# Cross-attention and mixture of experts: routed chunks of 64 tokens as two passes of 32 over four column tiles, the hidden block turned on VectorE

## What is computed

```python
x = x + xattn(layernorm(x), ctx, ctx, mask, ...)      # attention over 77 context rows
h = layernorm(x).reshape(-1, 256)
shared = (silu(h @ shared_gate) * (h @ shared_up)) @ shared_down
logits = h @ gate_w
topk_ids, topk_val = argmax(logits, -1), max(logits, -1)
xs = h * sigmoid(topk_val)[:, None]
# every token goes to the one expert e = topk_ids[token]
routed = (silu(xs @ routed_gate[e]) * (xs @ routed_up[e])) @ routed_down[e]
out = x + (shared + routed).reshape(x.shape)
```

## Time and profile before

| | |
|---|---|
| time, median of 3 runs | 328.64 us (328.41 to 329.23) |
| the profiled execution | 326.08 us, span of its instructions 324.1 us |
| granted TensorE clock | 0.982 of full speed over the span |
| TensorE busy | 89% of the span |
| VectorE, ScalarE, GpSimd busy | 39%, 27%, 16% |
| chain that ended last | TensorE 74%, VectorE 8%, issue 5% |

### The profile page before, as it was taken

One profiled execution on the slowest core, in us unless ns is written; L12 is line 12 of the kernel. 1 busy time (PEld: TensorE's weight loads), 2 busy tenths in 40 slices (PEclk: granted clock), 3 DMA queues, 4 the chain that ended last, 5 costly groups with the idle time before them and its releaser, 6 DMA issues.

```text
span 324.1 us, 7366 instructions
## 1 busy us (share of the span) xinstructions
PE 288.6 (89%) x2502; PEld 194.8 (60%) x2503; DVE 127.5 (39%) x402; ACT 88.2 (27%) x224; POOL 50.4 (16%) x88
## 2 busy tenths in 40 slices
PE   4968899987989999899999899989999989999760
PEld 3735665533834885567766676757776756764450
DVE  1648868773993211332223222222323222222423
ACT  2157764442211023322221222222222212221000
POOL 1245212110077400000000000000000000001772
PEclk9999999999999999999999999999999999999895
DMA  6999999000023351268885869999948995105475
GB/s 200 351 373 372 372 370 374 24 1 2 0 82 109 113 181 36 74 253 269 318 286 169 259 194 328 383 366 378 358 152 266 344 375 189 32 0 129 129 223 166
DMA packets 55148, 69.69 MB, mean 215 GB/s; under 512 B 4030, under 2 KB 37211, under 8 KB 55131
## 3 DMA queue, kind: packets, MB, share of 16 engines
q1 hardware_dynamic: 46203, 61.60, 55.7%
q10 hardware_dynamic: 7392, 3.67, 4.6%
q0 software_dynamic: 1536, 4.20, 4.2%
HBM read 59.49 MB, written 9.96 MB: 214 GB/s over the span
## 4 chain that ended last, share of the span: by engine, by line
PE 74%; DVE 8%; issue 5%; POOL 4%; DMA 3%; ACT 3%; ACTq 1%; POOLq 0%; SPq 0%; DVEq 0%
PE bank L991 29%; PE bank L1005 13%; PE bank L914 12%; PE bank L1015 6%; PE bank L926 4%; POOL xs_flat L436 4%; PE bank L845 3%; DMA slot_rows<-late 1%; DVE h_place L504 1%; PE bank L880 1%; DVE h_place L505 1%; ACT h_place L715 1%; DMA xs_flat<-slot_rows,slot_i 1%; DMA h_place<-in_L_xattn_kernel_q_dram 1%; PE bank L863 1%
## 5 line engine op out<-in xcount | busy, mean ns | idle before, releaser
L991 PE MATMUL bank<-ring_gu,h_place 128*64 128x256 f32 x784 | 95.4, 385 | 5.0 <-issue 4.5
L991 PEld LDWEIGHTS bank<-ring_gu,h_place 128*64 128x64 f32 x784 | 53.9, 136 | 34.8 <-issue 15.1
L616 DVE COPY h_place<-xs_flat 128x128 f32 x50 | 11.4, 227 | 104.2 <-PE bank L991 100.9
L1005 PE MATMUL bank<-ring_d,h_place 128*64 128x128 f32 x784 | 51.4, 273 | 0.5 <-ACT h_place L755 0.5
L1005 PEld LDWEIGHTS bank<-ring_d,h_place 128*64 128x64 f32 x784 | 46.6, 137 | 7.2 <-ACT h_place L755 0.8
L436 POOL DMA_INDIRECT xs_flat<-slot_rows,slot_i x16 | 15.6, 978 | 191.9 <-DMA slot_rows<-late 187.4
L755 ACT COPY h_place<-bank 128x256 f32<-128x256 f32 x49 | 18.2, 372 | 83.7 <-PE bank L1015 83.7
L926 PE MATMUL bank<-shd,h_place 128*128 128x256 f32 x128 | 30.0, 395 | 2.2 <-issue 2.2
L926 PEld LDWEIGHTS bank<-shd,h_place 128*128 128x128 f32 x128 | 25.3, 199 | 7.2 <-issue 3.5
L750 ACT ACTIVATE h_place<-bank 128x256 f32<-128x256 f32 x49 | 18.8, 383 | 38.8 <-PE bank L991 38.8
L914 PE MATMUL bank<-late,shg 128*128 128x512 f32 x48 | 23.1, 603 | 4.3 <-DVE h_place L505 4.2
(11 more groups left out here) (132 smaller groups left out, 246.9 us busy)
## 6 DMA issues: line engine op xcount, KB each, us to landing
ring_gu<-L_ffn_routed_gate_w_dram SPq DMA_DIRECT2D x32, 512.0 KB, 5.9
ring_gu<-n_L_ffn_routed_up_w_dram SPq DMA_DIRECT2D x32, 512.0 KB, 7.0
ring_d<-L_ffn_routed_down_w_dram SPq DMA_DIRECT2D x32, 512.0 KB, 6.6
slot_rows<-late ACTq DMA_DIRECT2D x14, 256.0 KB, 4.4
x<-in_x_dram SPq DMA_DIRECT2D x4, 512.0 KB, 7.1
slot_rows<-zeros SPq DMA_DIRECT2D x1, 2048.0 KB, 14.4
late<-sorted_rows SPq DMA_DIRECT2D x8, 256.0 KB, 3.4
out_dram<-x SPq DMA_DIRECT2D x8, 256.0 KB
```

The source lines that it names most:

```text
L991: ins = te.matmul(bank[w][a * LW:(a + 1) * LW, 0:FH], x_c[:, k], ring_gu[:, s, w, k, a * FH:(a + 1) * FH], start=(k == 0), stop=(k == KD - 1))
L1005: ins = te.matmul(bank[4][a * LW:(a + 1) * LW, 0:DH], hT[:, mp, mh * LW:(mh + 1) * LW], ring_d[:, s, m, a * DH:(a + 1) * DH], start=(m == ...
```

## The change

Gate/up is split by tokens: two passes u = 0, 1 of 32 tokens, each into a bank of its own, over four column tiles. Tile q gets the columns with index m * 128 + q * 32 + f (m = 0 to 3, f = 0 to 31) of gate and of up side by side, so that bank u holds on partition q * 32 + t the gate of token t in its left 128 columns and the up in the next 128. After silu and product on 128x128 blocks, a transposition within 32x32 blocks (VectorE, `turn`) gives `hT` with the hidden index on the partitions. The transposes on TensorE, bank 3 and the copy `keep_hT` go; ScalarE takes over `take_y`. Down runs as four column tiles of 32 (two halves of the output, two halves of the tokens). `x_c` stays a single buffer, `hT` too; `h_r` and silu's output have one buffer for each pass.

```diff
 def take_x(c):
     col = dve.value_load(begin[0:1, bass.ds(c, 1)], min_val=0, max_val=T)
-    dve.wait_ge(u_done, HALVES * c)
+    dve.wait_ge(gu_done, HALVES * c)
     v.tensor_copy(x_c, xsT[:, :, bass.ds(col, LW)]).then_inc(x_ready, 1)
-def gated(c):
-    dve.wait_ge(silu_done, c + 1)
-    dve.wait_ge(u_done, HALVES * (c + 1))
-    v.tensor_tensor(h_r, h_r, bank[1][:, 0:FH], ALU.mult).then_inc(h_ready, 1)
-def take_y(c):
-    dve.wait_ge(down_done, HALVES * (c + 1))
-    v.tensor_copy(y_all[:, bass.ds(c, 1)].rearrange("p c d -> p (c d)"), bank[4][:, 0:DH]).then_inc(y_ready, 1)
+def gated(c, u):
+    dve.wait_ge(silu_done, HALVES * c + u + 1)
+    v.tensor_tensor(h_r[u], g_silu[u], bank[u][:, P:2 * P], ALU.mult).then_inc(h_ready, 1)
+def turn(c, u):
+    dve.wait_ge(h_ready, HALVES * c + u + 1 + FREE2)
+    v.transpose(hT[:, :, u * LU:(u + 1) * LU],
+                h_r[u].rearrange("p (m f) -> p m f", m=KF)).then_inc(hT_ready, 1)
...
 with dve.Fori(1, n_chunks) as c:
+    for u in range(HALVES):
+        dve.wait_ge(hT_ready, HALVES * c + u - 1)
+        gated(c, u)
     take_x(c + 1)
-    gated(c)
-    take_y(c - 1)
-take_y(n_chunks - 1)
+    dve.wait_ge(down_done, c)
+    for u in range(HALVES):
+        turn(c, u)
...
 def silu(c):
-    act.wait_ge(g_done, HALVES * (c + 1))
-    act.wait_ge(hT_done, c)
-    a_.activation(h_r, bank[0][:, 0:FH], ACT.Silu).then_inc(silu_done, 1)
-def keep_hT(c):
-    act.wait_ge(hT_done, c + 1)
-    act.wait_ge(down_done, HALVES * c)
-    a_.copy(hT.rearrange(FLAT), bank[3][:, 0:FH]).then_inc(hT_ready, 1)
+    for u in range(HALVES):
+        act.wait_ge(gu_done, HALVES * c + u + 1)
+        act.wait_ge(h_ready, HALVES * c + u + 1)
+        a_.activation(g_silu[u], bank[u][:, 0:P], ACT.Silu).then_inc(silu_done, 1)
+def take_y(c):
+    act.wait_ge(down_done, c + 1)
+    a_.copy(y_all[:, bass.ds(c, 1)].rearrange("p c d -> p (c d)"), bank[4][:, 0:DH]).then_inc(y_ready, 1)
...
 def gate_up(c, s):
     pe.wait_ge(x_ready, c + 1)
-    for w, done in ((0, g_done), (1, u_done)):
+    columns = ring_gu[:, s].rearrange("p w k (m q f) -> p k q w m f", q=QUADS, f=LU)
+    for u in range(HALVES):
+        pe.wait_ge(h_ready, HALVES * c + u + 1)
         for k in range(KD):
-            for a in range(HALVES):
-                ins = te.matmul(bank[w][a * LW:(a + 1) * LW, 0:FH], x_c[:, k],
-                                ring_gu[:, s, w, k, a * FH:(a + 1) * FH],
+            for q in range(QUADS):
+                ins = te.matmul(bank[u][q * LU:(q + 1) * LU, 0:2 * P]...,
+                                x_c[:, k, u * LU:(u + 1) * LU], columns[:, k, q],
                                 start=(k == 0), stop=(k == KD - 1))
-                if k == KD - 1:
-                    ins.then_inc(done, 1)
+        ins.then_inc(gu_done, 1)
 def down_of(n, s):
-    pe.wait_ge(hT_ready, n)
+    pe.wait_ge(hT_ready, HALVES * n)
     pe.wait_ge(y_ready, n)
     for m in range(KF):
         for a in range(HALVES):
-            ins = te.matmul(bank[4][a * LW:(a + 1) * LW, 0:DH], hT[:, mp, mh * LW:(mh + 1) * LW], ...)
+            for u in range(HALVES):
+                r = a * LW + u * LU
+                ins = te.matmul(bank[4][r:r + LU, 0:DH], hT[:, m, u * LU:(u + 1) * LU], ...)
-def h_transposes(c):
-    pe.wait_ge(h_ready, c + 1)
-    for m in range(KF // HALVES):
-        ins = te.transpose(bank[3][:, m * P:(m + 1) * P], h_r[:, m * P:(m + 1) * P], ident[:])
-    ins.then_inc(hT_done, 1)
```

More of the change, by code:

```diff
@@ L41, in build_cross_attention_moe @@
     HALVES = 2
+    QUADS = 4
+    LU = P // QUADS
     LW = P // HALVES
@@ L194, in build_cross_attention_moe @@
         x_c = carve(P, KD, LW)
-        h_r = carve(P, FH)
-        hT = carve(P, KF // HALVES, P)
+        g_silu = [carve(P, P) for u in range(HALVES)]
+        h_r = [carve(P, P) for u in range(HALVES)]
+        hT = carve(P, KF, LW)
         y_t = xn
@@ L347, in _ @@
                     end = sp.value_load(chunk_end[0:1, bass.ds(e, 1)], min_val=1, max_val=MAX_CHUNKS)
-                    sp.wait_ge(u_done, HALVES * end)
+                    sp.wait_ge(gu_done, HALVES * end)
                     load_gate_up(e + RING, s)
-                    sp.wait_ge(down_done, HALVES * end)
+                    sp.wait_ge(down_done, end)
                     load_down(e + RING, s)
@@ L768, in _ @@
                 silu(j)
-                keep_hT(j)
+                if j:
+                    take_y(j - 1)
             with act.Fori(1, blocks) as b:
@@ L779, in _ @@
                 silu(c)
-                keep_hT(c)
+                take_y(c - 1)
+            take_y(n_chunks - 1)
             act.wait_ge(y_ready, STORE * blocks + FREE1)
@@ L987, in gate_up @@
                 pe.wait_ge(x_ready, c + 1)
-                for w, done in ((0, g_done), (1, u_done)):
+                columns = ring_gu[:, s].rearrange("p w k (m q f) -> p k q w m f", q=QUADS, f=LU)
+                for u in range(HALVES):
+                    pe.wait_ge(h_ready, HALVES * c + u + 1)
                     for k in range(KD):
-                        for a in range(HALVES):
-                            ins = te.matmul(bank[w][a * LW:(a + 1) * LW, 0:FH], x_c[:, k],
-                                            ring_gu[:, s, w, k, a * FH:(a + 1) * FH],
+                        for q in range(QUADS):
+                            ins = te.matmul(bank[u][q * LU:(q + 1) * LU, 0:2 * P].rearrange("p (w m f) -> p w m f", w=2, f=LU),
+                                            x_c[:, k, u * LU:(u + 1) * LU], columns[:, k, q],
@@ L993, in gate_up @@
                                             start=(k == 0), stop=(k == KD - 1))
-                            if k == KD - 1:
-                                ins.then_inc(done, 1)
+                    ins.then_inc(gu_done, 1)
             def down_of(n, s):
-                pe.wait_ge(hT_ready, n)
+                pe.wait_ge(hT_ready, HALVES * n)
                 pe.wait_ge(y_ready, n)
                 for m in range(KF):
-                    mh, mp = m // (KF // HALVES), m % (KF // HALVES)
                     for a in range(HALVES):
-                        ins = te.matmul(bank[4][a * LW:(a + 1) * LW, 0:DH], hT[:, mp, mh * LW:(mh + 1) * LW],
-                                        ring_d[:, s, m, a * DH:(a + 1) * DH],
-                                        start=(m == 0), stop=(m == KF - 1))
-                        if m == KF - 1:
-                            ins.then_inc(down_done, 1)
@@ L1011, in h_transposes @@
-            def h_transposes(c):
-                pe.wait_ge(h_ready, c + 1)
-                for m in range(KF // HALVES):
-                    ins = te.transpose(bank[3][:, m * P:(m + 1) * P], h_r[:, m * P:(m + 1) * P], ident[:])
-                ins.then_inc(hT_done, 1)
+                        for u in range(HALVES):
+                            r = a * LW + u * LU
+                            ins = te.matmul(bank[4][r:r + LU, 0:DH], hT[:, m, u * LU:(u + 1) * LU],
+                                            ring_d[:, s, m, a * DH:(a + 1) * DH],
+                                            start=(m == 0), stop=(m == KF - 1))
```

19 lines of the change are left out of this document (10 added, 9 removed).

## The result

The changed kernel takes **402.74 us** (median of 4 runs, 401.93 to 404.87) against 328.52 us of the kernel before, a ratio of 1.2264 (1.2211 to 1.2316). The forecast was 345.8 us, with a range up to 356: the direction was right, the size far off. The profiled execution took 404.87 us.

The account below looks back on a forecast made before the run. TensorE's own order bound the kernel; the way back through ScalarE and VectorE would then set 3.60 us intervals instead of 3.285. Profiled 326.08 + 14.8 + 0.5 + 1.9 = 343.3, put at the median: 345.8 us, range 336 to 356.

Parts of the forecast that it names:

- TensorE's part: TensorE in each interval: gate/up 1.77 us plus down at most 1.04, transposes gone; 2.81 us or a little less.
- The way back: From gate/up through ScalarE and VectorE to the next gate/up: 3.60 us, over TensorE's 2.81, so it sets the interval.
- steps 1 to 6: Gate/up to ScalarE 2.04, silu 0.27, to VectorE 0.03, product's dispatch to copy 0.88, copy 0.23, to TensorE 0.15 us.
- Block transposes at nothing: VectorE's two 128x128 block transposes per chunk, under TensorE's idle time and the next gate/up: no cost below about 0.85 us each.
- Start: Opening, chunk 0: second gate/up at 133.29 instead of 132.81, 0.5 us later.
- End: After the last gate/up: down starts 4.0 instead of 3.76 us later, last store 3.26 instead of 1.57 behind down; 1.9 us.
- Returns of the outer loop: TensorE's three returns: their idle 1.36 us lies behind down, within idle 0.8 and down's 1.04; 0 to 0.7 us each.
- "much slower" rival: Gate/up at half rate, TensorE's clock falling with an idle fifth, or block transposes over 0.85 us each; 388 to 427 us, chance 0.07.
- 388 and 427: Total us if VectorE's block transposes take 1.3 us each (388), or if gate/up's rate halves (427); together chance 0.07.

Follow-up runs that it names:

- ring of four: Changed kernel with four ring places instead of eight, the outer loop's text half as long and turning eight times: 347.55 us, ratio 1.0595 to the kernel before.
- ring of four with the copy moved: Changed kernel with four ring places and VectorE's copy of the next tokens put between a chunk's two products: 325.2 us, ratio 0.9842 to the kernel before.
- 1682: Loop instructions of the changed kernel with down as two column tiles of 64 tokens again, ring of eight: 378.7 us, ratio 1.1569 to the kernel before.
- 1102: Loop instructions of the changed kernel with four ring places instead of eight: 347.55 us, ratio 1.0595 to the kernel before.
- the old code in two laps: Kernel before with TensorE's outer loop written out for 16 experts instead of 8, two turns instead of four: 337.95 us, ratio 1.0278 to the kernel before.

## Why the prediction was wrong

**Right, by its steps.** *TensorE's part*: four column tiles run beside each other: the 32 passes of gate/up, 0.38 us each, take 1.93 us together, where 16 on two tiles took 1.95; down takes 1.06, and by themselves they can follow each other at 2.72 (ring of four with the copy moved), where 2.81 or less was said. *The way back*, steps 1 to 6: sum 3.60, measured 3.59 to 3.60 in the undisturbed intervals; its largest term, 0.88 from the dispatch of the second product to the copy, measured 0.93 (192.65 to 193.58), and with the load ahead of the product 0.20. That the load is what decides is shown, not argued: moving it alone gives 2.86 us. *Block transposes at nothing*: 287 ns each, two in 0.50 us, beside TensorE's gate/up. *Start*: 4.04 instead of 3.84, a loss of 0.2 where 0.5 was worked out. *End*: the last down started 368.25 - 364.32 = 3.93 behind its gate/up (4.0 said), and from its end to the span's end are 33.67 us instead of 32.13 - 0.07 = 32.06, 1.6 later where 1.69 was said. Four issues of stores in a row are there:

```profile
368.25 1.08 PE L1017 MATMUL bank<-ring_d,h_place 128*32 128x128 f32 x32 [1.12 <-DVE h_place L628]
...
369.83 3.68 ACTq L767 DMA_DIRECT2D slot_rows<-late  x4
```

**Wrong: one step.** "Returns of the outer loop: their 1.36 us lies behind down now ...; bounds 0 to 0.7 each, three times", and with it the silence on what stood under "TensorE's part": "Twice the count at twice the tiles is the same array time". The array time is the same, but the code is not. I counted what the doubled instructions cost when executed and not what they weigh as text. The returns cost 25 us with what follows them instead of 0 to 2, and stalls between them with the blocks at half rate behind them 33 more. With a text that is kept (ring of four) the returns are within those bounds: six of the seven have intervals of 3.69 to 3.75 us, 0.1 to 0.15 over the others. The rows that could have warned were in the trace of before: 11 packets on q8, and none behind 180 us, through two more returns. They say that this loop is kept, and leave open up to what size one is.

That a loop's text comes again belonged among the rivals, and none of them had it. The runs give its figures: at 2194 instructions 48 packets, branches back of 4.8 to 7.6 us and 55 us lost against the ring of four (402.74 - 347.55); at 1682 40 packets and 5.1 to 6.4 us; at 1102, 1209 and 1211 11 packets and 0.2 us.

**The clock.** The "much slower" rival named a falling clock, but by an idle fifth in each interval. That didn't happen: the ring of four idles 0.79 us in every 3.60 and has a granted clock of 0.983. It stood at half behind the long idle times (0.50 over the blocks at 202.41, 265.03, 312.95 and 329.63), and longer blocks make 19 us of the loss, most of it there (1.6 us are of the loop's second block, at half clock as well). The prices of that rival, 388 and 427, have the measured 402.74 between them; that is luck, since none of the causes that it named was at work.

**Left open.** No loop between 1211 instructions, kept, and 1682, fetched again, was run, so the size at which the one turns into the other wasn't bracketed closer. That the stalls between the returns are fetches too rests on their packets, 2.3 to 2.7 us ahead of each restart, and on the ring of four, where both go from the second lap on. In the first lap, in which the short texts have packets too, they stall as well: with a ring of four 0.65 us in the changed kernel (up to 149.60, the packet at 147.3) and 2.37 with the copy moved (up to 156.22, the packet at 153.7). Why some packets stall TensorE and others do not stays open.

## What to carry to other kernels

Before splitting instructions in a loop on one engine, count the loop's text on that engine and compare it with the packets of its instruction queue: here the loops with none from 3 us behind their first branch back on branched back in 0.2 us (1102, 1209 and 1211 instructions), and those with eight or more in every turn in 4.6 to 7.6 (1682 and more). A change that may take a loop from the one to the other needs a test of its own. If the text gets too long, write the largest block once and branch (1209 instructions instead of 2194, 337.2 us), and put register loads right behind a long dispatch, ahead of any instruction that waits (with one branch instead of two, 321.46). And when a copy is moved behind a product, its register load moves too: here that made 0.9 us in each interval, and putting it between the two products was worth 22 us on the ring of four.

## What the runs showed of the hardware

- **Fetching the loop again**: a branch back takes 4.6 to 4.7 us with the DMA queues at a share of 0.09 and 4.8 to 7.6 us in the changed kernel, beside the weights' transfers, against 0.2 us for a loop that is kept (1102, 1209 and 1211 instructions). The loops of 1682 instructions and more that were run have eight or more packets in every lap (cut at the first gate/up behind each return), and in the changed kernel a stall between the returns ends 2.3 to 2.7 us after the start of its packet. Packets on the instruction queue are 0.79 MB / 48 = 16.5 KB each; the kernel before has 11 in all, the old code in two laps 27 with its one return, the changed kernel 48 with three.
- **The clock after idling**: after every idle time of 5.3 us or more that I read, TensorE came back with a block of 3.2 to 3.64 us (1.93 undisturbed) at a granted clock of 0.50 to 0.59 over the block, 0.50 in most. After 1.36 us (a block of 1.95) and after 2.63 us (at 253.85, a block of 1.93) it was 1.00; after 2.83 us (at 178.12, a block of 3.36) it was 0.56, so the length of the idle time alone doesn't tell between these. Even the same wait ends both ways: at the loop's second block the changed kernel came back from 2.11 us with a block of 3.56 at 0.53, the same kernel with a ring of four from 2.12 us with one of 1.93 at 1.00.
- **Down on tiles of 64 between gate/ups on tiles of 32** made the interval 0.16 us longer than down on tiles of 32 (2.88 against 2.72), 0.11 from gate/up to down and 0.06 from down to gate/up. The change of tile and the halved count of down's matmuls went in together.
- **The register load behind a product that waits** on VectorE started with the product and not in the wait ahead of it: in the changed kernel VectorE is idle for 0.58 us ahead of the second product (192.65), the load starts at 192.8 and takes 0.305 us, and the copy starts 0.93 us behind the product. With the load ahead of the product (ring of four; it starts at 171.8, the product at 172.54) the copy starts 0.20 behind it.
